# A gated block with top-1 experts: expert weight transfers issued from GpSimd's queue instead of SyncE's

## What is computed

```python
x = x + tanh(g_xattn) * xattn(ctx, layernorm(x))     # linear attention, few projections
s = layernorm(x)                                      # input of the second block
q, k, v = s@Wq+bq, s@Wk+bk, s@Wv+bv                   # 16 heads of 16 features
a = softmax(q k^T / 4) v                              # per batch and head, 512 x 512 scores
y = layernorm(s + a@Wo + bo) * ln1_g + ln1_b
e = floor(y @ router_w + router_b) mod 4              # one expert of four per token
f = relu(y @ W1[e] + b1[e]) @ W2[e] + b2[e]           # W1 256x1024, W2 1024x256
out = x + tanh(g_ffn) * (layernorm(y + f) * ln2_g + ln2_b)
```

## Time and profile before

| | |
|---|---|
| Median of 3 runs | 580.56 us (577.52 to 580.72) |
| The profiled execution's own time | 580.17 us |
| Its span in the profile | 578.1 us |
| PE busy | 482.5 us, 83% of the span |
| DVE busy | 390.9 us, 68% |
| ACT busy | 244.9 us, 42% |
| POOL busy | 207.4 us, 36% |
| Queue q1 (SP) | 34272 packets, 38.37 MB |
| Queue q0 (POOL) | 5328 packets, 15.74 MB |
| Mean granted clock of PE | 0.87 of full |

### The profile page before, as it was taken

One profiled execution on the slowest core, in us unless ns is written; L12 is line 12 of the kernel. 1 busy time (PEld: TensorE's weight loads), 2 busy tenths in 40 slices (PEclk: granted clock), 3 DMA queues, 4 the chain that ended last, 5 costly groups with the idle time before them and its releaser, 6 DMA issues. The chain is left out here.

```text
span 578.1 us, 8313 instructions
## 1 busy us (share of the span) xinstructions
PE 482.5 (83%) x2535; PEld 278.8 (48%) x2535; DVE 390.9 (68%) x871; ACT 244.9 (42%) x483; POOL 207.4 (36%) x273
## 2 busy tenths in 40 slices
PE   3985999989999999999987789864289998988960
PEld 2542443343334444433422332213289888988960
DVE  4655579796789895789798698017966555555651
ACT  1021016563445462446566254453055444544530
POOL 3153005030025124034033375412345555555651
PEclk9996779998989986989999795557579999998995
DMA  7637521643474523437647800200111211111220
GB/s 222 141 94 254 132 33 43 244 139 94 78 109 169 195 85 103 108 44 182 190 110 189 159 21 1 76 0 1 54 37 36 64 56 54 55 40 53 64 54 19
DMA packets 40127, 54.99 MB, mean 95 GB/s; under 512 B 12686, under 2 KB 24476, under 8 KB 40093
## 3 DMA queue, kind: packets, MB, share of 16 engines
q1 hardware_dynamic: 34272, 38.37, 26.7%
q0 software_dynamic: 5328, 15.74, 8.5%
q10 hardware_dynamic: 492, 0.47, 0.3%
HBM read 36.73 MB, written 17.83 MB: 94 GB/s over the span
## 5 line engine op out<-in xcount | busy, mean ns | idle before, releaser
L588 ACT ACTIVATE probs<-sc 128x512 f32<-128x512 f32 x256 | 141.4, 595 | 173.1 <-PE sc L892 170.1
L736 DVE TENSOR_REDUCE mx<-amax 128x1 f32<-128x512 f32 x256 | 166.6, 678 | 47.2 <-PE amax L883 47.1
L892 PE MATMUL sc<-QS,KS 50*128 50x512 f32 x256 | 108.1, 502 | 14.9 <-ACT probs L588 12.5
L883 PE MATMUL amax<-KS,QS 48*128 48x512 f32 x256 | 106.9, 500 | 11.0 <-DMA KS<-qk_dram 6.2
L892 PEld LDWEIGHTS sc<-QS,KS 50*128 50x128 f32 x256 | 43.7, 202 | 115.9 <-ACT probs L588 56.1
L883 PEld LDWEIGHTS amax<-KS,QS 48*128 48x128 f32 x256 | 42.0, 197 | 28.0 <-DVE mx L736 13.8
L1247 PE MATMUL amax<-W_hi,hid_hi 128*128 128x256 f32 x160 | 48.2, 301 | 4.2 <-DVE hid_lo L1147 3.8
L526 POOL TENSOR_TENSOR an<-av,rec 128x256 f32<-128x256 f32 x16 | 10.2, 637 | 102.8 <-DVE rec L725 102.7
L1247 PE MATMUL amax<-W_hi,hid_lo 128*128 128x256 f32 x160 | 46.7, 292 | 0.0
L1247 PE MATMUL amax<-W_lo,hid_hi 128*128 128x256 f32 x160 | 46.5, 291 | 0.0
L904 PE MATMUL pv<-probs,V1b 128*32 128x512 f32 x256 | 44.8, 780 | 1.4 <-ACT probs L588 1.2
(11 more groups left out here) (220 smaller groups left out, 897.0 us busy)
## 6 DMA issues: line engine op xcount, KB each, us to landing
qk_dram<-HL SPq DMA_DIRECT2D x16, 512.0 KB, 3.9
QS<-qk_dram SPq DMA_DIRECT2D x90, 64.0 KB, 3.2
KS<-qk_dram SPq DMA_DIRECT2D x90, 64.0 KB, 3.1
W_sb<-in_L_ffn_W SPq DMA_DIRECT2D x8, 512.0 KB, 4.3
xc<-in_x SPq DMA_DIRECT2D x4, 512.0 KB, 3.6
xc<-in_ctx SPq DMA_DIRECT2D x4, 512.0 KB, 4.6
x_dram<-xc POOLq DMA_DIRECT2D x4, 512.0 KB, 3.5
res_dram<-t_a POOLq DMA_DIRECT2D x4, 512.0 KB, 3.9
```

Source lines behind the costliest of these rows:

```text
L588: nc.scalar.activation(probs[:, n % 8, c * 512:(c + 1) * 512], sc[c][:, :], ACT.Exp, scale=SCALE).then_inc(exp_done, 1)
L736: nc.vector.reduce_max(mx[:, to:to + 1], amax[m % 3][:, :], AX.X).then_inc(max_done, 1)
L883: nc.tensor.matmul(amax[m % 3][:, :], QS[rows, pair, chunk * P:(chunk + 1) * P], KS[rows, pair, :], start=True, stop=True).then_inc(A_full, 1)
L892: nc.tensor.matmul(sc[c][:, :], KS[rows, pair, kc * P:(kc + 1) * P], QS[rows, pair, :], start=True, stop=True).then_inc(sc_full, 1)
```

## The change

The issues of the 16 weight pieces and of b1 and b2 leave SP's program and stand in POOL's, at the same half-steps, behind the GPSIMD table's work of that half-step and ahead of a split there. Sizes, destinations, semaphores and waits stay as they were. POOL's transfers go out on q0. The two functions keep their bodies but for the engine.

```diff
             for u in range(BEGIN, END):              # SP's program
                 ...
-                if u in FIRST_LAYERS:
-                    load_first(FIRST_LAYERS[u] // KD, FIRST_LAYERS[u] % KD)
-                if u in SECOND_LAYERS:
-                    load_second(SECOND_LAYERS[u] // 2, SECOND_LAYERS[u] % 2)
...
+            def load_first(e, k):
+                pool.dma_start(W1_sb[:, e * KD + k, :], W1[e, k * P:(k + 1) * P, :]).then_inc(w_early if e < 1 else w2_loaded, 16)
+
+            def load_second(e, half):
+                if e == 0 and half == 0:
+                    for s, v in ((x1_stored, B * 16), (src_done, B * TT), (cT_full, B * 2), (t1_done, B * 2), (csum_done, B * 2),
+                                 (Q_full, B * 2), (V_full, B * 2), (Y_full, B * 2)):
+                        pool.wait_ge(s, v)
+                    pool.dma_start(b1_col[:, :], b1.rearrange("e (f p) -> p (e f)", p=P), allow_slow_non_contiguous=True).then_inc(w2_loaded, 16)
+                    pool.dma_start(b2_bc[:, :, :], b2.partition_broadcast(P)).then_inc(w2_loaded, 16)
+                n = NF // 2
+                pool.dma_start(W2_sb[e][:, half * n:(half + 1) * n, :], W2[e, half * n * P:(half + 1) * n * P, :].rearrange("(k p) d -> p k d", p=P)).then_inc(w_early if e < 2 else w2_loaded, 16)
...
             for u in range(BEGIN, END + OVER):       # POOL's program
                 for b, what in at(GPSIMD, u):
                     ...
+                if u in FIRST_LAYERS:
+                    load_first(FIRST_LAYERS[u] // KD, FIRST_LAYERS[u] % KD)
+                if u in SECOND_LAYERS:
+                    load_second(SECOND_LAYERS[u] // 2, SECOND_LAYERS[u] % 2)
                 if u in SPLITS:
                     split_early(*EARLY[SPLITS[u]])
```

More of the change, by code:

```diff
@@ L376, in sp_program @@
                 load_stack(0, g)
[L378 to L389, removed]
             for u in range(BEGIN, END):
```

## The result

The changed kernel took 588.96 us (median of 4 runs, 585.64 to 591.65) where the kernel before, on the same chip, took 579.04 us (4 runs, 576.44 to 580.72). The ratio is 1.0162, with a 95% interval of 1.0116 to 1.0208: **slower**, by about 9 us. I had said 579.0 us and "no change". The profiled execution after took 587.69 us; its span is 585.7 us, 7.6 us more than before.

The account below looks back on a forecast made before the run. PE, busy 83% of the span, was taken to set the pace in the attention loop. Terms of -1.85, -0.87, +0.87 and +0.5 summed to -1.35 us, 578.8 from the profile or 579.2 from the median; forecast 579.0 us, range 571.5 to 588.

Parts of the forecast that it names:

- First term: Second batch's k rows, near 128: without W(28) on SP, store 3 lands sooner and PE's stand goes; -1.85 us, bounds 0 and -1.85.
- Second term: Maxima of half-step 184, PE's stand at 311.02: without W(174) between, the fetch comes 0.93 us earlier; -0.87 us.
- Third term: Fourth batch's stack rows, stand at 321.54: SP starts 1.37 us sooner, a third transfer costs +1.4; net +0.87, bounds -4.08 and +2.3.
- What moves onto others: Costs on POOL and shared DMA engines: W(164) with W(174) beside the maxima of 168, +0.5 us; POOL's own issues 0.
- The clock, which had a rival of its own: PE's granted clock, about half in two stretches before, might shift: faster around 571 us (0.12), slower around 588 us (0.10).
- the prediction's own signs of being wrong: Last stand vanishing, b1's issue over 14 us, or the clock from 130 on differing from before.
- b1: POOL's issue of 4096 single elements after half-step 144's layernorm step: taken as 6.5 us, hidden; other end 32 us, +18 us.
- rival (c): b1's issue blocks POOL at 267.26, delaying DVE's transpose at 287.73 and PE's maxima: up to +18 us, 597 us; chance 0.09.
- POOL's own 14 us: About 0.8 us of POOL for each of 17 transfers of 512 KB, hidden in its waits for DVE; cost 0.
- (b): Pairs W(164) with W(174) and W(184) with W(194) collide: +2 and +2.3 us, first two terms 0; 584.5 us, chance 0.09.
- (a): Nothing won: all queues share the DMA engines, only SP's issue time is saved; 580.2 us, chance 0.20.
- (d): PE's granted clock moves with what PE did just before: faster around 571 us, chance 0.12; slower around 588 us, chance 0.10.

Follow-up runs that it names:

- The quiet versions: Kernels with all weight and bias issues at moments when PE does not wait for SP's small transfers, on SP or POOL; ratios to the kernel before 0.9833, 0.9837, 0.9916.
- e7: Kernel before, all issues kept on SP's queue but moved to quiet moments; ratio to the kernel before 0.9833, 577.53 us.
- e12: Repeat, unaltered, of the kernel with all issues on POOL's queue at quiet moments; ratio to the kernel before 0.9916, 574.15 us.
- e2: Changed kernel with the eight W1 pieces back on SP, only W2, b1 and b2 on POOL; ratio to the kernel before 1.0352, 595.82 us.
- e5: Kernel before, all issues on SP's queue but at the moments when POOL issued them after the change; ratio to the kernel before 1.0165, 590.76 us.
- e8: Changed kernel, all issues on POOL's queue but moved to quiet moments; ratio to the kernel before 0.9837, 577.96 us.

## Why the prediction was wrong

Step by step, as it was put.

**First term (-1.85 us, the stand near 128).** The transfer went as said: POOL issues W(28) at 102.11 (forecast 102.28), and store 3 to k rows is 3.05 us (118.29 to 121.34, issue to issue) where the earlier trace rows had 5.27. The stand is gone. But PE won 0.89 us of the 1.85: twice it waits for DVE's maxima right behind (0.37 and 0.47 us). What is late next was not asked. The prediction's price of a weight issue on SP, 0.40 to 0.51 us, left out the 0.90 us of W(174) in the earlier trace rows; nothing hangs on it.

**Second term (-0.87 us, the fetch of 184).** The step itself was right: 312.37 to 314.34, 1.97 us as forecast, with no W(174) between. PE's stand there is 1.90 us all the same, for the same maxima, where 0.87 was to go to nothing. The work ahead of it had been shifted; I have not followed which part.

**Third term (the stand at 200, 3 to 5 us).** It is 3.81 us. The +1.4 us for a third transfer beside the rows came: the stand ends 7.3 us behind the last row's issue (321.57 to 328.90), where it was 5.9. The net +0.87 did not, because PE came to the rows later, 3.5 us behind that issue instead of 1.8. That the stand was right within 3 to 5 us is therefore in part luck. The quiet versions, which take the second pair from there, leave 0.47 (e7) to 2.26 us (e12).

**"What moves onto others" is the step that failed.** It put +0.5 us, bounds 0 and +2, on the pair W(164) and W(174), and it looked only at the maxima of 168. Even there it was too low: their fetch took 3.5 us longer (5.48 instead of 1.96), against 0.93 to 2. The k rows of the same batch, issued beside the pair, were not in it. Worse, b1, b2, W(144) and W(154) were counted as POOL's time only and never as traffic in front of the maxima of 152: the prediction followed POOL's queue for what POOL pays and not for what SP's transfers meet. Measured: a swing of 9.96 us between half-steps 168 and 176. The removal runs give the biases and the pair about 3 us each of the stand of 7.05. The clock, which had a rival of its own and no term, differs from 130 on (0.76 instead of 0.52 from 212 to 226, 0.50 within the stand): that was one of the prediction's own signs of being wrong.

**b1.** Its issue took 1.78 us where I had 6.5 (bounds to 32): rival (c) did not happen, and DVE's transpose of the earlier trace rows, now at 283.67, does not wait for `an`. The Trainium skill (DMA: Bandwidth & Descriptors, Rules for kernel authors) has one descriptor for each element here. On SP's queue the trace agrees: 4112 packets under 512 B from 263 to 267 in the kernel before. On POOL's no count shows it; if there were 4096 of them, each took POOL 0.43 ns by my estimate. By the Trainium skill's remark that many descriptors can be emitted before their cost shows (DMA: Bandwidth & Descriptors, Anatomy of one DMA) the issue should be cheap, and the trace agrees with its 1.78 us.

**POOL's own 14 us.** Hidden, as said: the two tight places named are still waits for DVE (5.82 us ahead of 323.02, 2.72 us ahead of 363.31), and an issue costs 0.75 to 0.85 us for a W2 piece.

**The rivals.** (b) had the kind right (pairs collide) and its bounds too small: 584.5 us, "still within 1%", against 588.96. (a) was right on the mechanism: no queue keeps transfers apart. It erred at 123.80: the 2.28 us did go (3.05 instead of 5.27 us), and W(28) had left 16 us earlier, which is again the moment; with W(28) back on SP (e2) the stand is back. e5 beside the change (1.0165 and 1.0162) shows it, and e7 beside e8 (0.9833 and 0.9837) fits it. By the Trainium skill (DMA: Bandwidth & Descriptors, Issuing engines are not separate DMA queues) transfers of all issuers interleave on the same engines; the trace agrees (transfers of both queues at 288 to 290, the engines at 1.07, SP's k rows late behind POOL's pair). But (a) took "same engines" to mean "no loss", and that does not follow: the moments change too. (d) gave 588 us for one more slow stretch, tied to no stand. One came, but in the stand, so it should have been tied to (b) and not kept as a case apart. That its 588 us lies beside the 588.96 measured is luck: its slow stretch was priced at 7 us, and the one that came cost some 4 beside a stand that (d) did not have.

## What to carry to other kernels

- Moving an issue to another engine at "the same half-step" moves it in time. Work out between which two waits of the new engine it goes out; everything between two waits goes out together, here as pairs of 512 KB.
- Price a bulk transfer by the small transfers that it meets and for which the critical engine waits, also those that are only the first of a chain (maxima, stores, q rows, k rows here). A store and its fetch took 1.96 us with nothing bulky beside them and 3.7 (e5, maxima of 168) to 9.0 us (e12, maxima of 136) in company.
- When one stand is taken away, look for the next collision before counting the gain, and use a ruler of equal work units in both traces instead of the whole time.

## What the runs showed of the hardware that was not expected

POOL's issue of 4096 single elements took 1.78 us, that of 512 rows of 1 KB 0.75 to 0.85 us. The same 8.93 MB were 9632 packets on q1 and 2528 on q0. From 266 to 270, while b1's elements were moved, the DMA engines were 0.70 busy at 40 GB/s; from 288 to 290 they were full at 328 GB/s. On SP's queue the issue of b2 behind b1 held the queue for 2.47 us (e5), on POOL 0.56. And the granted clock stayed at half for 12 to 42 us behind stands of 1.82 to 7.05 us, with PE busy 91 to 94% of the time in the stretches at half, but only for some 4 us behind the stand of 4.08 us in the kernel before.
